# Linear attention: head sums in 32-column pieces, expert scores with the centroids as weights for six of eight batches, and the second expert weight fetched in six loads

## The reference, cut to what matters

```python
# layer 0, attention (16 heads of 16 features), h = modulated layernorm of x
q, k = elu(q) + 1, elu(k) + 1
kv    = einsum('bnhd,bnhm->bhdm', k, v)
k_sum = k.sum(axis=1)
out   = einsum('bnhd,bhdm->bnhm', q, kv) / (einsum('bnhd,bhd->bnh', q, k_sum) + EPS)
x     = x + ga * (out @ Wproj.T + bproj)
# layer 0, experts: each token goes to the expert with the highest score
aff    = h2 @ centroids.T                 # 8 experts
assign = argmax(aff, axis=1)
ye     = xs + relu(layernorm(xs) @ w1[e].T + b1[e]) @ w2[e].T + b2[e]
```

## Time and profile before

| | |
|---|---|
| median of three runs (lowest, highest) | 1079.24 us (1075.13, 1080.31) |
| profiled execution | 1079.79 us, its span 1078.0 us |
| PE busy | 980.7 us, 91% of the span, 10611 matmuls |
| DVE, ACT, POOL busy | 58%, 45%, 36% |
| second expert weight, one load of 8.4 MB | issued at 218.99 us, landed 25.2 us later |
| last small load (`b2`, 1 MB) | issued at 224.31 us, landed 24.9 us later |
| first `up` of the experts | begins at 251.65 us, 13.44 us after `tok_i` |

### The profile page before, as it was taken

The page is one execution under the profiler, slowest core; times in us unless marked ns, Lnnn a source line. Parts: engine busy times, 40 slices in busy tenths (PEclk is TensorE's granted clock), DMA queues, the critical chain, the costliest instruction groups (busy, mean ns, idle before and its releaser), DMA issues. The chain is left out here.

```text
span 1078.0 us, 28845 instructions
## 1 busy us (share of the span) xinstructions
PE 980.7 (91%) x10611; PEld 844.5 (78%) x10612; DVE 624.5 (58%) x1457; ACT 484.2 (45%) x1308; POOL 383.5 (36%) x341
## 2 busy tenths in 40 slices
PE   6899999986999999999987899999767799899996
PEld 3567666876999999999976777777656698799995
DVE  2477777772445444444421678898886678244442
ACT  2655464202454454445345767677662350222221
POOL 0534334511222222322112455556552100455552
PEclk9999999988999999999998899999966559999999
DMA  9874531285222222222045666666521530444441
GB/s 336 264 275 131 143 131 40 79 357 191 97 89 81 89 89 91 83 89 73 17 94 83 116 123 148 135 130 119 109 76 56 213 149 2 147 134 141 138 135 34
DMA packets 132283, 135.49 MB, mean 126 GB/s; under 512 B 73788, under 2 KB 122046, under 8 KB 130644
## 3 DMA queue, kind: packets, MB, share of 16 engines
q1 hardware_dynamic: 120948, 90.80, 30.0%
q0 software_dynamic: 11232, 43.27, 12.4%
HBM read 96.21 MB, written 44.77 MB: 131 GB/s over the span
## 5 line engine op out<-in xcount | busy, mean ns | idle before, releaser
L938 PE MATMUL psall<-rows 128*128 128x128 f32 x1872 | 223.2, 276 | 2.2 <-DVE rows L992 2.2
L938 PEld LDWEIGHTS psall<-rows 128*128 128x128 f32 x1872 | 216.6, 193 | 2.9 <-issue 2.8
L905 POOL DMA_INDIRECT x<-ffn_rows,tok_i x78 | 82.0, 1051 | 249.4 <-DVE rows L1011 148.6
L992 DVE COPY rows<-wlo 128x2048 f32 (+1 forms) x78 | 75.2, 964 | 113.8 <-PE psall L938 101.3
L950 PE MATMUL psall<-whi,rows 128*128 x624 | 141.0, 379 | 0.0
L950 PEld LDWEIGHTS psall<-whi,rows 128*128 128x128 f32 x624 | 115.7, 190 | 14.1
L1249 DVE STREAM_TRANSPOSE whi<-whi 32x512 f32<-32x512 f32 x128 | 89.8, 701 | 9.1 <-POOL whi L1212 7.7
L1051 ACT ACTIVATE rows<-psall,rows 128x128 f32<-128x128 f32 x312 | 84.9, 383 | 10.8 <-PE psall L938 7.2
L1330 ACT ACTIVATE whi<-psall 32x512 f32<-32x512 f32 x128 | 75.2, 588 | 29.9 <-PE psall L1459 25.7
L910 POOL DMA_INDIRECT attn_rows<-rows,tok_i x39 | 39.5, 1014 | 120.3 <-DVE rows L1024 120.3
L1202 POOL TENSOR_TENSOR whi<-whi,cst 128x512 f32<-128x512 f32 x32 | 40.7, 1271 | 98.7 <-ACT whi L1330 98.7
(11 more groups left out here) (227 smaller groups left out, 1732.0 us busy)
## 6 DMA issues: line engine op xcount, KB each, us to landing
ffn_rows<-mod_rows SPq DMA_DIRECT2D x2, 4096.0 KB
wlo<-in_W SPq DMA_DIRECT2D x2, 4096.0 KB, 17.3
whi<-mod_rows SPq DMA_DIRECT2D x4, 1024.0 KB, 14.1
ffn_rows<-rows SPq DMA_DIRECT2D x8, 512.0 KB
ffn_rows<-x SPq DMA_DIRECT2D x8, 512.0 KB
wlo<-attn_rows SPq DMA_DIRECT2D x32, 128.0 KB, 3.3
v_turn<-wlo SPq DMA_DIRECT2D x32, 128.0 KB, 2.7
wlo<-v_turn SPq DMA_DIRECT2D x32, 128.0 KB, 3.8
```

The costliest lines, as they stand in the source:

```text
L905: eng.indirect_dma_start(xin[j % DEEP], None, src_d, bass.IndirectOffsetOnAxis(tok_i[:, j:j + 1].bitcast(U32), 0), bounds_check=T, oob_is_ ...
L938: last = eng.matmul(b_up[t.par][f // 4][:, (f % 4) * P:(f % 4 + 1) * P], w_now[:, c, f * P:(f + 1) * P], inT[t.par][:, c * P:(c + 1) * P], ...
L992: eng.tensor_copy(w_now, w_up[:, bass.ds(e, 1)].rearrange("p o c n -> p (o c) n")).then_inc(e_["w"], 1)
```

## The change

1. `kv_sum` makes 32×33 blocks instead of 128×129: for each half, each token tile and each of four groups `q` of 32 features, the weights are 32 features of k, the moving operand is the same 32 features of v and a ones column. That is 32 written matmuls for 8. The four groups write four ranges of 32 partitions. ACT's copy of v (`keep_kv`) writes groups of 33 columns, and `mask_kv` reads the 32 columns four times through a broadcast.
2. `score` of batches 0 to 5 swaps its operands: the 8 centroids are the weights, 128 tokens are the moving operand, and the four token tiles write four ranges of 32 partitions. ACT copies the result to `affT` (`keep_turned_scores`, four copies of 8×128), PE turns it with one transpose in the next step (`turn_scores`), and ACT then copies the turned scores to `key` (`early_scores`). Batches 6 and 7 keep the old way.
3. The second expert weight comes in six loads: experts 0, 1 and 2 (1 MB each) after the stores of batches 1, 3 and 5, expert 4 after those of batch 6 (with waits for the last `kv_proj` and the last gate product), and expert 3 (1 MB) and experts 5 to 7 (3 MB) where the one load stood.

```diff
-        vs = sbuf("vs", TB * C * (P + 1))
+        vs = sbuf("vs", TB * C * 4 * 33)
+        def scored(b):
+            return 2 * b + 2 if b < B - 2 else B - 2 + b + 1
+        def load_w2(eng, e, count=1):
+            part = slice(e * F0 // P * D, (e + count) * F0 // P * D)
+            eng.dma_start(whi[:, part], a["w2"][:, part]).then_inc(s_w2, 16)
...
+                if b in (1, 3, 5):
+                    load_w2(eng, b // 2)
+                if b == 6:
+                    eng.wait_ge(ev["kv"], B * TB)
+                    eng.wait_ge(ev["pre"], 3 * B)
+                    load_w2(eng, 4)
...
-                    eng.tensor_tensor(kvm[c][:, 0:P], ps[2 + c][:, 0:P], blocks, ALU.mult)
+                    eng.tensor_tensor(kvm[c][:, 0:P].rearrange("p (q n) -> p q n", q=4), bc_mid(ps[2 + c][:, 0:32], 4),
+                                      blocks.rearrange("p (q n) -> p q n", q=4), ALU.mult)
...
             def keep_scores(b):
-                eng.wait_ge(ev["aff"], b + 1)
+                eng.wait_ge(ev["aff"], scored(b))
...
+            def keep_turned_scores(b):
+                if b < B - 2:
+                    eng.wait_ge(ev["aff"], scored(b) - 1)
+                    for k in range(TB):
+                        last = eng.activation(affT[32 * k:32 * k + E, :], ps[0][32 * k:32 * k + E, 0:P], ACT.Copy)
+                    last.then_inc(ev["affc"], 1)
...
                 for c in range(C):
                     for k in range(TB):
-                        last = eng.matmul(ps[2 + c][:, 0:P + 1], fk3[:, k, c * P:(c + 1) * P], vs4[:, k, c, :], start=k == 0, stop=k == TB - 1)
+                        for q in range(4):
+                            last = eng.matmul(ps[2 + c][32 * q:32 * q + 32, 0:33], fk3[:, k, c * P + 32 * q:c * P + 32 * q + 32], vs4[:, k, 4 * c + q, :],
+                                              start=k == 0, stop=k == TB - 1)
...
+                if b < B - 2:
+                    for c in range(C):
+                        for k in range(TB):
+                            last = eng.matmul(ps[0][32 * k:32 * k + E, 0:P], cent[:, c, :], o0T[:, c, k * P:(k + 1) * P], start=c == 0, stop=c == C - 1)
+                    last.then_inc(ev["aff"], 1)
+                    return
...
+            def turn_scores(b):
+                if b < B - 2:
+                    eng.wait_ge(ev["affc"], b + 1)
+                    eng.transpose(ps[0][:, P:2 * P], affT, ident).then_inc(ev["aff"], 1)
...
-            eng.wait_ge(ev["aff"], B)
-            eng.dma_start(whi[:, :], a["w2"]).then_inc(s_w2, 16)
+            eng.wait_ge(ev["aff"], scored(B - 1))
+            load_w2(eng, 3)
+            load_w2(eng, 5, 3)
```

More of the change, by code:

```diff
@@ L90, in two_layer_kernel @@
         eps_t = sbuf("eps_t", 1)
+        affT_t = sbuf("affT", P)
         idx = [sbuf(f"idx{i}", 1, I32) for i in range(2)]
@@ L336, in attn0_vector @@
             ch.put(eng.memset(vs[:, :], 1.0))
+            ch.put(eng.memset(affT, 0.0))
             eng.wait_ge(s_e, 1)
@@ L561, in stage @@
                         wait_some(eng, ev["oT"], b)
-                    eng.activation(vs4[:, k, :, 0:P], ps[k % 2][:, D:2 * D].rearrange("p (c n) -> p c n", c=C), ACT.Copy)
+                    eng.activation(vs4[:, k, :, 0:32], ps[k % 2][:, D:2 * D].rearrange("p (q n) -> p q n", n=32), ACT.Copy)
                     eng.activation(fk3[:, k, :], ps[k % 2][:, 0:D], ACT.Exp)
@@ L581, in keep_scores @@
             def keep_scores(b):
-                eng.wait_ge(ev["aff"], b + 1)
-                eng.activation(key[:, b * TB * E:(b + 1) * TB * E], ps[0][:, 0:TB * E], ACT.Copy).then_inc(ev["key"], 1)
+                eng.wait_ge(ev["aff"], scored(b))
+                scores = ps[0][:, P:2 * P].rearrange("p (k n) -> p k n", k=TB)[:, :, 0:E] if b < B - 2 else ps[0][:, 0:TB * E].rearrange("p (k n) -> p k n", k=TB)
+                eng.activation(key3[:, b * TB:(b + 1) * TB, :], scores, ACT.Copy).then_inc(ev["key"], 1)
@@ new lines, in keep_turned_scores, with early_scores, late_scores @@
+            def keep_turned_scores(b):
[4 more added lines that the diff above has]
+                    last.then_inc(ev["affc"], 1)
+            def early_scores(b):
+                if b < B - 2:
+                    keep_scores(b)
+            def late_scores(b):
+                if b >= B - 2:
+                    keep_scores(b)
@@ L585, in attn0_scalar @@
             rstd_h = rstd_of(3, lambda b: b + 1)
-            batch_steps([(AFTER_QKV, exp_q), (AFTER_O, copy_oT), (AFTER_QKV, relu_q), (AFTER_QKV, second_mods), (AFTER_QKV, keep_kv(0)), (AFTER_QKV, keep_kv(1)),
+            batch_steps([(AFTER_QKV, exp_q), (AFTER_H + 1, early_scores), (AFTER_O, copy_oT), (AFTER_QKV, relu_q), (AFTER_QKV, second_mods), (AFTER_QKV, keep_kv(0)), (AFTER_QKV, keep_kv(1)),
                          (AFTER_N, norm_x), (AFTER_N, first_mods), (AFTER_H, rstd_h), (AFTER_QKV, keep_kv(2)), (AFTER_QKV, keep_kv(3)),
-                         (AFTER_H, copy_hT), (AFTER_N, shift_h), (AFTER_O, rstd_of(2, lambda b: b + 1)), (AFTER_H, keep_scores),
+                         (AFTER_H, copy_hT), (AFTER_N, shift_h), (AFTER_O, rstd_of(2, lambda b: b + 1)), (AFTER_H, keep_turned_scores),
@@ L695, in idle_last @@
                 return lambda b: hold_clock(eng, times, ps[2][:, 0:P]) if b == B - 1 else None
-            batch_steps([(AFTER_QKV, q_proj), (AFTER_QKV, second_mods), (AFTER_O, turn_o), (AFTER_QKV, kv_proj((0, 1))), (AFTER_O, project),
+            batch_steps([(AFTER_QKV, q_proj), (AFTER_QKV, second_mods), (AFTER_H + 1, turn_scores), (AFTER_O, turn_o), (AFTER_QKV, kv_proj((0, 1))), (AFTER_O, project),
                          (AFTER_QKV, kv_proj((2, 3))), (AFTER_H, turn_h), (AFTER_N, turn_n), (AFTER_QKV, kv_sum), (AFTER_H, score), (AFTER_QKV, attend)],
-                        [(AFTER_O, idle(10)), (AFTER_O, turn_o), (AFTER_O, idle(5)), (AFTER_O, project), (AFTER_H, idle_last(10)), (AFTER_H, turn_h),
+                        [(AFTER_H + 1, turn_scores), (AFTER_O, idle(10)), (AFTER_O, turn_o), (AFTER_O, idle(5)), (AFTER_O, project), (AFTER_H, idle_last(10)), (AFTER_H, turn_h),
                          (AFTER_H, idle(5)), (AFTER_H, score)])
```

20 lines of the change are left out of this document (12 added, 8 removed).

## The result

| | before | changed |
|---|---|---|
| median (lowest, highest) | 1079.40 us (1075.13, 1080.31), 4 runs | 1061.97 us (1060.36, 1063.69), 4 runs |
| profiled execution, its span | 1079.79, 1078.0 us | 1063.0, 1061.2 us |

The ratio is 0.9836, 95% interval 0.9813 to 0.9859: 17.4 us less. Run again later it took 1062.31 us (5 runs), ratio 0.9845 (0.9831 to 0.9860).

The account below looks back on a forecast made before the run. PE was taken to bound layer 0 attention, and the late `b2` load the layer 0 experts' start. Savings of 8.9 + 6.9 = 15.8 us gave 1064.0 or 1063.4, so 1063.7 us; range 1060 to 1071.5.

Parts of the forecast that it names:

- (a): Layer 0 attention: narrow matmuls have a floor per instruction, so `kv_sum` stays as long as now; 1070.5 us, chance 0.13.
- (b): Layer 0 experts don't start earlier, because another small load or the weight's rest is still last; 1070.5 us, chance 0.12.
- (c): Both (a) and (b) at once: 2.2 us saved, 1077 us, chance 0.04.
- (d): Slower: narrow weight loads don't overlap, so each `kv_sum` record costs 0.11 us; 1113 us, chance 0.03.
- (e): Better: `early_scores` and the copies cost PE nothing and the gather is a microsecond quicker; 1060 us, chance 0.08.
- `kv_sum` to `attend`: Layer 0 attention, PE: the distance between these starts falls from 3.56 to 1.91 us, with `mask_kv` last.
- `kv_proj` waits for `key`: Layer 0 attention: PE waits 0.38 us a step for ACT's copy of turned scores; the transpose adds 0.11.
- Steps 5 to 9: Layer 0 attention: each saves 1.65 us less 0.11 for the transpose and 0.38 for the wait, net 1.16 us.
- Steps 2 and 3: Layer 0 attention, where `score` is missing: 0.84 us saved each, of which step 2 keeps 0.59 because of POOL's gate product.
- Part 1: Narrow sums and swapped scores in layer 0 attention: 8.9 us saved in all.
- The pause: Layer 0 experts, `tok_i` to first `up`: 7.82 us instead of 13.44 once `b2` lands earlier, 5.62 us saved.
- The clock of the first `up`: Layer 0 experts: the first `up` runs at full clock after a shorter pause, 1.3 us saved (bounds 0 and 1.3).

Follow-up runs that it names:

- the reordered kernel: The changed kernel with `turn_scores` ahead of `q_proj` on PE and `early_scores` ahead of `exp_q` on ACT; 1059.31 us, in its second run 1057.72 us.
- small loads first: The kernel before with the four small loads issued ahead of the one load of the second expert weight; 1081.38 us, ratio 1.0013.
- attention only: The changed kernel with the second expert weight in one load again, as before the change; 1067.56 us, ratio 0.9881.

## Why the prediction held, step by step

The time came out 1.7 us under the forecast of 1063.7, and rivals (a) to (d) fell. So did (e), though its 1060 is as near: the wait for `key` was there, and the pause was 7.8 us. That the forecast came so near is partly the cancelling of terms.

- **`kv_sum` to `attend`, predicted 1.91 us.** Measured 1.74. The mis-sized term is `kv_sum`: 1.18 us (64 × 17 ns and 0.1) against 0.56 to the next row and 0.75 with its tail, 9 ns a record instead of 17. The 17 were taken over from a row with 64 moving columns, though here there are 33. That row and its neighbour with 128 columns and 28 ns have the same order, the four output ranges in turn, so over the three forms (28, 17 and 9 ns for 128, 64 and 33 columns) the price falls with the columns. So rival (a), a floor of 28 ns, is refuted. The rule that I set beside it (the Trainium skill, TensorEngine Tiling (Array Packing), section Instruction Overhead: about 60 cycles for each matmul) would be an estimated 25 ns at full clock. The trace gives 9 with neighbours on different output ranges and 20 on the same one, so it doesn't hold for this form. The faster sum bought little, as the prediction's two other chains said: `shift_h` (put at 1.69) ends the wait in steps 4 to 8, not `mask_kv` as I wrote.
- **`kv_proj` waits for `key`, predicted 0.38, with 0.11 for the transpose.** From `q_proj` to `kv_proj` it is 129.39 − 124.59 = 4.80 us; with the transpose moved away it is 107.19 − 102.88 = 4.31. Together 0.49, as predicted.
- **Steps 5 to 9, predicted 1.16 each.** Measured 1.13, by two errors that cancel. The faster sum gave 0.17 more, and 0.20 went to two things that I hadn't charged there. One is 0.09 us where PE goes from the turns to the narrow weights (119.08 to 120.92, 1.84, against 100.73 to 102.48, 1.75, with wide weights in the kernel with swapped scores alone); I had this at 0.1, but inside `kv_sum`. The other is 0.11 from `kv_proj` to `project`, 3.54 behind the wait for `key` and 110.62 − 107.19 = 3.43 where that wait is gone, so the wait costs 0.5 us and not 0.38.
- **Steps 2 and 3, predicted 0.84 each before POOL's wait.** Measured 2.75 − 1.48 = 1.27, by the same mis-sized `kv_sum`. POOL's gate product is late in step 2 as predicted. Part 1 in all: 9.3 us against 8.9 (10.3 in the second execution, with the shorter waits at the start).
- **The pause, predicted 7.82.** Measured 7.82, 7.91 and 7.74 in three kernels that have the six loads. The size was taken from layer 1 and is right. The reason was half right: I named `b2`, which was last before, but the gathers were behind the same bytes, and with `b2` ahead of the whole weight nothing was gained. `b2` landed at 228.3, 2.0 us ahead of `tok_i`.
- **The clock of the first `up`, predicted 1.3 us.** This step failed. The first `up` took 5.09 and 6.21 us in two executions of the changed kernel, 0.19 and 1.31 more than before instead of 1.3 less. It isn't that the kernel can't have it: the weight loads alone, and three more runs, had 3.57 to 3.58. The row of layer 1 from which I took full clock is itself only one outcome, as the same place there shows, where both kernels have the same code; the changed kernel, then the reordered kernel's second run:

```profile
900.36 0.41 PE L980 MATMUL psall<-cst,x 128*128 128x128 f32 x2 [1.30 <-DMA x<-ffn_rows,tok_i]
902.28 0.44 PE L980 MATMUL psall<-cst,x 128*128 128x128 f32 x2 [1.51 <-DMA x<-ffn_rows,tok_i]
902.56 2.79 PE L990 MATMUL psall<-rows 128*128 128x128 f32 x16
```

```profile
897.62 0.41 PE L980 MATMUL psall<-cst,x 128*128 128x128 f32 x2 [1.36 <-DMA x<-ffn_rows,tok_i]
899.52 0.44 PE L980 MATMUL psall<-cst,x 128*128 128x128 f32 x2 [1.49 <-DMA x<-ffn_rows,tok_i]
899.79 1.95 PE L990 MATMUL psall<-rows 128*128 128x128 f32 x16
```

  The pauses agree to 0.06 us, and 16 records are busy 2.79 us once and 1.95 once. The prediction gave bounds of 0 and 1.3 us and put the upper one into its sum; what was measured lies below both. Why the clock is lower in one execution and not in another stays open.
- **What was not in the prediction.** The plan took 0.88 us more in the profiled run, because more of the idle matmuls ahead of it ran at half clock (68 in 9.73 us); the second run has 42.63, as before, so it isn't the change's. And about 2.6 us net came from layer 1, whose code is untouched. There the same 6016 to 6017 matmuls of attention were busy 251.4 us in the changed kernel and 256.6 before, at a granted clock of 0.89 and 0.87. Over all profiled runs layer 1 attention takes 305.3 to 307.2 us with the old layer 0 attention (three runs), 304.8 and 305.5 with one of its two edits, and 301.5 to 306.0 with both. The ranges overlap; the expectation that the first profile's 301.9 would repeat missed (303.30); and with the second run of the reordered kernel it was 304.5. Layer 1's experts go with the clock at their own start: in the seven executions where their first `up` ran at full clock (1.79 us to the next turn) they take 163.7 to 164.0 us, in the seven others 164.8 to 166.5, with either code ("small loads first" has the old one and 166.36). Whether the change moves these stages at all stays open.

The median's gain, 17.4 us, is therefore some 15 us in the two places that the prediction named (9.3 and 5.6), and a rest of 2 to 3 us that goes with PE's clock and that no run ties to the change. The forecast had 15.8 with 1.3 us that didn't come, and this rest, which it didn't have, took their place: that is luck. The parts alone give 12.8 and 7.8 us, 3.2 more than 17.4 together; 1.4 of that is the pause, which shortened in "attention only" as well, and the rest is within the intervals of the three ratios.

## What to carry to other kernels

When a product is wanted only in its diagonal blocks, many narrow matmuls can cost less than a few wide ones: put neighbours on different output ranges, price them from a row of the same weight form, loop order and number of moving columns, and expect the gain to stop at the next chain: of 3.56 us from `kv_sum` to `attend` 1.74 stayed, though `kv_sum` itself takes 0.56. A large load whose result is needed late can delay small transfers that are needed early, here on its own queue and on another: split it, and ask for each piece when its place becomes free. A term that depends on the clock behind a pause should be a bound in the sum, not a value, until several executions have shown the same.

## What the runs showed of the hardware that I had not expected

- A float32 matmul record with 32-column weights and 33 moving columns costs 9 ns, weights included, when its neighbours write other ranges of output partitions, and 20 ns when they write the same and add to the same sum; only the order of the loops differs.
- A gather on POOL's queue that takes 4.4 us by itself took 11.0 us while an 8.4 MB load was under way on SP's queue, and ended with it.
- In two executions of one program (the reordered kernel) PE's pauses ahead of the first `up` were 1.25 and 1.35 us, and 1.10 and 1.40; its granted clock in the two microseconds behind them was 0.50 in the first and 1.00 in the second.
- With twice the narrow matmuls PE stopped four times in one execution, for 2.1 to 5.0 us, with no waker in the profile.
